# Steps of older images placed from written tables, one ring of four PSUM banks, and the second halves of the turned attention rows copied by VectorE

## The chip, the cores and the metric

The kernel runs on one core of a Trainium2 chip. The metric is the device time of one execution in microseconds (us). Three executions of the kernel before took 2924.77, 2925.54 and 2934.96 us; the median is 2925.54 us.

## What is computed

Eight images x of 128 channels and 32 x 32 points pass through six layers, each added to its input:

```python
x = x + deform_conv2d(_gn(x))          # group norm, 3x3 taps sampled at learned offsets
x = x + attention_conv(_gn(x))         # 1024 x 1024 attention, small q and k
t = to_tokens(x)                       # 1024 tokens of 128 channels
t = t + attention(_ln(t))              # scores + fractional log bias, softmax
t = t + experts(_ln(t))                # 8 experts, top 2 shares: gelu(t W1 + b1) W2 + b2
t = t + linear_attention(_ln(t))       # 16 heads, normed k and v, projection, gelu
t = t + experts(_ln(t))
```

All is float32. One image is one sequence of 1024 tokens, which the kernel holds as 8 tiles of 128 tokens.

## The kernel before

**Images overlap.** `period(m, p)` runs ten times (p from 0 to 9). In it image p, the front, goes through the deformable convolution (`sampling`), its projections (`mid0`), attention 1, `mid1` and attention 2. Beside it run *side steps* of older and of the next image: `experts(..., 0, ...)` (layer 2's experts, called A here) and `gating` of image p-1, `layer3`, `gating` B and `experts` B of image p-2, and `start` (group norm, offsets, the hat tables) of image p+1. From p = 2 to p = 6 all of them are there; in the periods 8 and 9 there is no front.

**Hooks.** The front's code calls `side(n)` at numbered places, the hooks. G hooks 0 to 52 lie in sampling (0 to 39) and `mid0` (40 to 52); X hooks 0 to 77 lie in attention 1 (0 to 32, three for each row tile j), `mid1` (33 to 44) and attention 2 (45 to 77). Each engine (PE, DVE, ACT, POOL, SP) has its own program with the same hooks and does its own share of a step there, so the order on every engine is written out; there is no scheduler. The list `..._PLACES[n]` names the steps at hook n. `placed` spreads the steps evenly between anchors.

**Experts.** A step of `experts` is a product into one PSUM bank (`hidden`, L820) with a gelu by ACT (L1077); at every odd step from 3 on also `outputs` (L830, 16 matrix instructions), which DVE weighs and adds to the tokens (L1404).

**An attention row tile j.** PE computes 128 x 1024 scores into a bank pair (L796), DVE takes the maximum (`nmax`, L1365), ACT the exponentials (`prob`, L1061). Two tiles later PE transposes them in two halves (`turn`, L780), ACT copies each half out of bank `pt` (`keep_turned`, L1047) and three tiles later PE multiplies by the values (`weigh`, L788). Gelu and exponential need different activation tables: an ACT_TABLE_LOAD stands at each change.

**Banks.** Four banks are shared, `pt`, `pv`, `3a` and `3b`. `shared_banks` goes through the hooks once and gives each product the bank that was used longest ago; in the X hooks only three, `pv`, `3a` and `3b`, since `pt` is kept for `turn`. PE waits in `claim` until the last reader of the bank has released it:

```python
def turn(j, h):
    claim("pt")
```

**Sampling.** 18 halves n = 2k, 2k+1 of 9 taps k. For each half the DMA queue of SP loads y hats into slot n % 4 of `dist`, and for each tap x hats into slot k % 2 of `prob`, four DMAs each; DVE multiplies them (`multiplied`, L1267); PE contracts the product with weighted image chunks (L670). DVE multiplies half n+1 before it goes through the two hooks of half n. `next_hats(m, n)` on SP waits until PE has used half n, asks for y hats n+4, and for odd n then waits for DVE's half n and asks for x hats of tap k+2.

## Time and profile before

| | |
|---|---|
| three runs | 2924.77 / 2925.54 / 2934.96 us |
| profiled execution, its own time | 2928.26 us |
| its span on the core | 2926.4 us |
| mean granted TensorE clock | 0.938 of full |
| busy PE / DVE / ACT | 2368.4 / 1429.6 / 1343.8 us |

The span is what the trace covers, from the first instruction to the last; 1.9 us of the profiled execution lie around it. An engine's busy time is the union of its instructions, so span less busy time is idle time, and a row in square brackets or a row of the waits says which instruction of which engine ended an idle stretch.

### The profile page before, as it was taken

The page shows a single profiled execution, that of the slowest core. Times are in us where ns is not written, and L with a number is a line of the kernel's source. Part 1 is how long each engine was busy: PE and PEld are TensorE (multiplying, and loading weights), DVE is VectorE, ACT ScalarE, POOL GpSimd, SP SyncE. Part 2 cuts the span into 40 slices and gives each one's busy share as a digit, 9 for nine tenths or more (in the row PEclk, how much of TensorE's full clock was granted, in tenths as well). Part 3 has the DMA queues.
Part 4 walks back from the last instruction along what each step waited for, and adds up shares of the span by engine and source line. Part 5 has one row for each costly group of instructions (what it writes and reads, how often), then busy time and mean ns, then how long its engine had stood idle before and what let it go on. Part 6 is the DMA issues. An engine that isn't in the chain of part 4 may idle for free.

```text
span 2926.4 us, 36546 instructions
## 1 busy us (share of the span) xinstructions
PE 2368.4 (81%) x12672; PEld 1738.2 (59%) x12672; DVE 1429.6 (49%) x3543; ACT 1343.8 (46%) x1784; POOL 93.8 (3%) x87
## 2 busy tenths in 40 slices
PE   4677787778978888787888888887897888977958
PEld 2555565566656665665656666566665666655646
DVE  2345345564446535465444644456453653455352
ACT  2135163426473365625565264742747337543323
POOL 0000000000000000000000000000000000000000
PEclk8889998989999999999999999998999999998979
DMA  8603600440005200170002600044000530000000
GB/s 276 140 1 87 152 1 7 119 113 1 1 37 137 73 1 8 53 174 13 1 15 80 145 8 1 29 108 109 1 1 37 136 67 1 1 8 1 1 8 8
DMA packets 106607, 157.88 MB, mean 54 GB/s; under 512 B 14896, under 2 KB 88720, under 8 KB 105872
## 3 DMA queue, kind: packets, MB, share of 16 engines
q1 hardware_dynamic: 104544, 142.39, 19.4%
q10 hardware_dynamic: 1840, 12.71, 1.1%
q8 instruction: 117, 1.92, 0.3%
q14 instruction: 106, 0.87, 0.1%
HBM read 126.76 MB, written 28.28 MB: 53 GB/s over the span
## 4 chain that ended last, share of the span: by engine, by line
PE 51%; ACT 16%; DVE 12%; ACTq 7%; issue 5%; DVEq 3%; DMA 3%; SPq 2%; PEld 0%; POOL 0%; PEldq 0%; POOLq 0%
PE pair L820 10%; PE pair L830 10%; PE pair L788 7%; PE pair L670 4%; ACT L1077 4%; ACT L1061 4%; ACTq L1063 4%; PE pair L657 3%; ACT dist L1047 3%; PE pair L780 3%; DMA prob<-hats 3%; ACTq L1078 3%; PE pair L603 2%; PE pair L617 2%; PE pair L796 2%
## 5 line engine op out<-in xcount | busy, mean ns | idle before, releaser
L670 PE MATMUL pair<-dist,thirds 128*128 128x256 f32 (+6 forms) x1440 | 315.6, 368 | 79.4 <-DVE dist L1267 71.7
L788 PE MATMUL pair<-vt,dist 128*128 128x128 f32 x2048 | 274.7, 291 | 90.5 <-ACT hiddenA L1077 45.3
L670 PEld LDWEIGHTS pair<-dist,thirds 128*128 128x128 f32 x1440 | 262.3, 209 | 136.9 <-DVE dist L1267 61.9
L788 PEld LDWEIGHTS pair<-vt,dist 128*128 128x128 f32 x2048 | 259.8, 205 | 118.1 <-issue 108.3
L830 PEld LDWEIGHTS pair<-wtsb,hiddenB 128*128 128x128 f32 x2048 | 251.8, 194 | 78.3 <-issue 50.5
L1077 ACT ACTIVATE hiddenB<-pair,wtsb 128x512 f32<-128x512 f32 x256 | 175.7, 687 | 257.0 <-PE pair L820 251.8
L820 PE MATMUL pair<-tnTB,wtsb 128*128 128x512 f32 x512 | 267.5, 617 | 30.4 <-ACT hiddenB L1077 26.8
L830 PEld LDWEIGHTS pair<-wtsa,hiddenA 128*128 128x128 f32 x2048 | 250.6, 194 | 67.7 <-issue 60.5
L820 PE MATMUL pair<-tnTA,wtsa 128*128 128x512 f32 x512 | 277.1, 634 | 9.8 <-ACT hiddenA L1077 6.2
L1077 ACT ACTIVATE hiddenA<-pair,wtsa 128x512 f32<-128x512 f32 x256 | 176.0, 687 | 223.4 <-PE pair L820 213.1
L1404 DVE SCALAR_TENSOR_TENSOR tokC<-pair,cwb,tokC 128x128 f32<-128x128 f32 x512 | 144.3, 345 | 262.6 <-PE pair L830 260.7
L1047 ACT ACTIVATE dist<-pair 128x512 f32<-128x512 f32 x256 | 152.9, 597 | 248.8 <-PE pair L780 236.0
L830 PE MATMUL pair<-wtsb,hiddenB 128*128 128x128 f32 x2048 | 253.3, 277 | 15.7 <-ACTq L1078 15.7
L830 PE MATMUL pair<-wtsa,hiddenA 128*128 128x128 f32 x2048 | 252.5, 277 | 0.1
L1267 DVE TENSOR_TENSOR dist<-dist,prob 128x1024 f32<-128x1024 f32 x144 | 174.6, 1223 | 135.6 <-DMA prob<-hats 113.9
L1365 DVE TENSOR_REDUCE nmax<-pair 128x1 f32<-128x1024 f32 x128 | 156.6, 1224 | 162.7 <-PE pair L796 161.0
L1404 DVE SCALAR_TENSOR_TENSOR tokD<-pair,cwa,tokD 128x128 f32<-128x128 f32 x448 | 126.2, 345 | 223.5 <-PE pair L830 222.7
L780 PE MATMUL pair<-early_sb,prob 128*128 128x128 f32 x1024 | 163.4, 282 | 65.7 <-ACT dist L1047 58.8
L993 ACT ACTIVATE thirds<-pair 128x768 f32<-128x768 f32 x96 | 77.9, 811 | 273.6 <-PE pair L657 273.2
L780 PEld LDWEIGHTS pair<-early_sb,prob 128*128 128x128 f32 x1024 | 120.1, 144 | 115.3 <-ACT dist L1047 100.8
L1061 ACT ACTIVATE prob<-pair,nmax 128x1024 f32<-128x1024 f32 x128 | 142.7, 1115 | 42.1 <-DVE nmax L1365 38.8
L1077 ACT ACT_TABLE_LOAD x120 | 154.0, 1283 | 16.1 <-issue 15.2
(193 smaller groups left out, 2923.8 us busy)
## 6 DMA issues: line engine op xcount, KB each, us to landing
dist<-hats SPq DMA_DIRECT2D x576, 128.0 KB, 3.3
prob<-hats SPq DMA_DIRECT2D x288, 128.0 KB, 3.4
hats<-dist SPq DMA_DIRECT2D x40, 512.0 KB, 2.7
ximg<-x SPq DMA_DIRECT2D x8, 512.0 KB, 3.8
result<-xo ACTq DMA_DIRECT2D x8, 512.0 KB, 3.9
hats<-prob SPq DMA_DIRECT2D x5, 608.0 KB, 15.0
late_sb<-late ACTq DMA_DIRECT2D x1, 2737.5 KB, 12.5
wtsa<-wa ACTq DMA_DIRECT2D x1, 2056.0 KB, 18.5
```

Of the source, the lines that this page charges most:

```text
L670: last = pe.matmul(pair[0][:, a:b], z[k // 3 % 2][:, c, k % 3, :], rhs(a, b), start=bank not in opened, stop=final, skip_group_check=True)
L780: last = pe.transpose(psum["pt"][:, t * P:(t + 1) * P], pr[j % 3][:, (4 * h + t) * P:(4 * h + t + 1) * P], ident)
L788: last = pe.matmul(psum[bank][:, 0:P], prT[j % 2][:, t, :], vt[:, t, :], start=(t == 0), stop=(t == NT - 1))
L820: pe.matmul(psum[bank], w[:, at_:at_ + P], xT[:, h * 512:(h + 1) * 512], start=True, stop=True)\
L830: last = pe.matmul(psum[bank][:, j * P:(j + 1) * P], hid[l][2 * (u % 2) + c][:, j * P:(j + 1) * P], w[:, at_:at_ + C], start=(c == 0), sto ...
L1047: released(act.activation(to, psum["pt"], ACT.Copy), "pt")
L1061: released(act.activation(pr[j % 3], pair[j % 2][:, :], ACT.Exp, bias=nmax[:, j:j + 1], accum_out=rsum[:, j:j + 1]), str(j % 2))
L1063: act.drain().then_inc(sem("prob_exp"), 1)
L1077: released(act.activation(hid[l][2 * (u % 2) + c], psum[bank], ACT.Gelu, bias=wts[l][:, at_:at_ + 1]), bank)
L1267: dve.tensor_tensor(slot, slot, windows(k, half), ALU.mult).then_inc(sem("hat_ready"), 1)
L1365: dve.tensor_reduce(nmax[:, j:j + 1], pair[j % 2][:, :], AX.X, ALU.max, negate=True)\
L1404: last = dve.scalar_tensor_tensor(to[:, t, :], psum[bank][:, j * P:(j + 1) * P], cw[l][:, t, e:e + 1], src[:, t, :], ALU.mult, ALU.add)
```

## The change

Four things are changed. The arithmetic is the same.

1. `placed` takes a written table: the hook of each step, one by one. Some steps now share a hook, and some stretches have none. `EARLY_EXPERTS` goes from 10 to 11: one more step of experts A lies in the G hooks.
2. The ring in the X hooks has all four banks, and the two halves of each turned tile take theirs from it, as every other product does.
3. The second half of each turned tile is copied by DVE, after the hook 3j+1, and no more by ACT.
4. In sampling DVE multiplies up to two halves ahead, by the table `MULTIPLY_AT` (entry i is the half n at which half i is multiplied), and SP asks for the x hats of tap k+2 before the y hats of half n+4.

```diff
+MULTIPLY_AT = [-1, 0, 0, 1, 2, 3, 4, 6, 6, 8, 8, 9, 10, 12, 13, 14, 15, 16]
+RING = ("pt", "pv", "3a", "3b")
+KEEP = ("act", "dve")
...
-def placed(anchors, hooks):
-
-    at = [[] for _ in range(hooks)]
-    for (s0, h0), (s1, h1) in zip(anchors, anchors[1:]):
-        for step in range(s0, s1):
-            at[h0 + (step - s0) * (h1 - h0) // (s1 - s0)].append(step)
-    return at
+def placed(first, at, hooks):
+
+    return [[first + n for n, h in enumerate(at) if h == hook] for hook in range(hooks)]
...
-EARLY_EXPERTS = 10
-EXPERTS_A_G_PLACES = placed([(0, 38), (EARLY_EXPERTS, G_HOOKS)], G_HOOKS)
-EXPERTS_A_PLACES = placed([(EARLY_EXPERTS, 0), (EXPERT_STEPS, 34)], X_HOOKS)
+EARLY_EXPERTS = 11
+EXPERTS_A_G_AT = [32, 34, 34, 40, 40, 42, 43, 46, 46, 51, 52]
+EXPERTS_A_G_PLACES = placed(0, EXPERTS_A_G_AT, G_HOOKS)
+EXPERTS_A_AT = [1, 2, 3, 3, 3, 3, 3, 8, 8, 8, 15, 16, 18, 19, 21, 22, 24, 24, 25, 26, 29, 31, 32]
+EXPERTS_A_PLACES = placed(EARLY_EXPERTS, EXPERTS_A_AT, X_HOOKS)
...
             for step in places[n]:
-                take(("pv", "3a", "3b"), claims(thread, l, step))
+                take(RING, claims(thread, l, step))
         for a, first in enumerate((0, ATTENTION2_AT)):
             i, r = divmod(n - first, 3)
             if r == 0 and 3 <= i < NT + 3:
-                take(("pv", "3a", "3b"), [("pv", a, i - 3)])
+                take(RING, [("pv", a, i - 3)])
+            if r < 2 and 2 <= i < NT + 2:
+                take(RING, [("turned", a, i - 2, r)])
...
             def next_hats(m, n):
 
-                if n + SLOTS < HALVES:
-                    sp.wait_ge(sem("hat_used"), at(m, HALVES, n + 1))
-                    load_hy(m, n + SLOTS)
                 k = n // 2
                 if n % 2 and k + 2 < TAPS:
                     sp.wait_ge(sem("hat_ready"), at(m, HALVES, n + 1))
                     load_hx(m, k + 2)
+                if n + SLOTS < HALVES:
+                    sp.wait_ge(sem("hat_used"), at(m, HALVES, n + 1))
+                    load_hy(m, n + SLOTS)
...
                 def turn(j, h):
-                    claim("pt")
+                    bank = SHARED["turned", a, j, h]
+                    claim(bank)
...
                 multiplied(0)
                 for n in range(HALVES):
-                    if n + 1 < HALVES:
-                        multiplied(n + 1)
+                    for later_half in range(1, HALVES):
+                        if MULTIPLY_AT[later_half] == n:
+                            multiplied(later_half)
...
+                def keep_turned(j, h):
+                    dve.wait_ge(sem("prob_T"), inst(m, a, 2 * NT, 2 * j + h + 1))
+                    if h == 0:
+                        dve.wait_ge(sem("pv"), inst(m, a, NT, j + 1))
+                    to = prT[j % 2][:, 4 * h:4 * h + 4, :].rearrange("p a b -> p (a b)")
+                    bank = SHARED["turned", a, j, h]
+                    released(dve.tensor_copy(to, psum[bank]), bank)
+                    dve.drain().then_inc(sem("probT_kept"), 1)
...
                     side(3 * j + 1)
+                    if KEEP[1] == "dve" and 2 <= j < NT + 2:
+                        keep_turned(j - 2, 1)
```

**ACT in the middle of attention 1.** The names: `prob` is the exponential, `hiddenA` a gelu of experts A, `dist` the copy of a turned half. Before:

```order
L1061 ACT_TABLE_LOAD
L1061 ACTIVATE prob,rsum<-pair,nmax 128x1024
L1077 ACT_TABLE_LOAD
L1077 ACTIVATE hiddenA<-pair,wtsa 128x512 x2
L1047 ACTIVATE dist<-pair 128x512 x2
L1061 ACT_TABLE_LOAD
L1061 ACTIVATE prob,rsum<-pair,nmax 128x1024
L1077 ACT_TABLE_LOAD
L1077 ACTIVATE hiddenA<-pair,wtsa 128x512 x2
L1047 ACTIVATE dist<-pair 128x512
L1077 ACTIVATE hiddenA<-pair,wtsa 128x512
L1047 ACTIVATE dist<-pair 128x512
```

Each tile has two table loads, two gelus and two copies. After the change (line numbers are those of the changed file):

```order
L1072 ACTIVATE prob,rsum<-pair,nmax 128x1024
L1088 ACT_TABLE_LOAD
L1088 ACTIVATE hiddenA<-pair,wtsa 128x512 x3
L1058 ACTIVATE dist<-pair 128x512
L1072 ACT_TABLE_LOAD
L1072 ACTIVATE prob,rsum<-pair,nmax 128x1024
L1058 ACTIVATE dist<-pair 128x512
L1072 ACTIVATE prob,rsum<-pair,nmax 128x1024
L1088 ACT_TABLE_LOAD
L1088 ACTIVATE hiddenA<-pair,wtsa 128x512
L1058 ACTIVATE dist<-pair 128x512
L1088 ACTIVATE hiddenA<-pair,wtsa 128x512
```

The copies of second halves are gone, three gelus stand together, and between the last two exponentials of the piece there is no gelu and no table load.

**PE at the start of `mid0`.** L576 (now L585) is the group product that waits for DVE's statistics, L583 (now L592) the q and k projections, L820 and L830 (now L830 and L840) are experts A. Before:

```order
L576 MATMUL pair<-gstF,early_sb 128x1
L617 MATMUL pair<-early_sb,tnB 128x128 x4
L820 MATMUL pair<-tnTA,wtsa 128x512 x2
L830 MATMUL pair<-wtsa,hiddenA 128x128 x8
L576 MATMUL pair<-gstF,early_sb 128x1
L858 MATMUL pair<-late_sb,tnTB 128x8 x4
L820 MATMUL pair<-tnTA,wtsa 128x512 x2
L830 MATMUL pair<-wtsa,hiddenA 128x128 x8
L583 MATMUL pair<-xrows,early_sb 128x512 x2
L820 MATMUL pair<-tnTA,wtsa 128x512
L583 MATMUL pair<-xrows,early_sb 128x512 x2
```

After:

```order
L840 MATMUL pair<-wtsa,hiddenA 128x128 x8
L830 MATMUL pair<-tnTA,wtsa 128x512
L585 MATMUL pair<-gstF,early_sb 128x1
L626 MATMUL pair<-early_sb,tnB 128x128 x4
L830 MATMUL pair<-tnTA,wtsa 128x512
L840 MATMUL pair<-wtsa,hiddenA 128x128 x8
L585 MATMUL pair<-gstF,early_sb 128x1
L868 MATMUL pair<-late_sb,tnTB 128x8 x4
L830 MATMUL pair<-tnTA,wtsa 128x512 x2
L840 MATMUL pair<-wtsa,hiddenA 128x128 x8
L830 MATMUL pair<-tnTA,wtsa 128x512
L592 MATMUL pair<-xrows,early_sb 128x512 x4
```

An outputs product and a hidden product now stand right ahead of the first group product (and one hidden product more ahead of this piece); two hidden products, an outputs product and a third hidden one stand right ahead of the projections, all four of which follow each other.

**DVE in the first half of sampling.** L1480 (now L1505) takes keys and values of the linear attention out of PSUM, L1487 to L1499 (now L1512 to L1524) norm them, L1267 (now L1278) multiplies hats. Before:

```order
L1448 TENSOR_TENSOR tnTF<-tnTF,late_sb 128x256
L1450 TENSOR_TENSOR tnTF<-tnTF 128x256
L1452 TENSOR_REDUCE cwa<-tnTF 128x32
L1454 SCALAR_TENSOR_TENSOR cwa<-cwa,lga 128x32
L1487 TENSOR_REDUCE hm<-hiddenA 128x128
L1267 TENSOR_TENSOR dist<-dist,prob 128x1024
L1458 COPY cwTa<-pair 64x128
L1494 TENSOR_SCALAR hm<-hm 128x256
L1496 RECIPROCAL hm<-hm 128x256
L1499 TENSOR_TENSOR qk<-qk,hm 128x1024
L1267 TENSOR_TENSOR dist<-dist,prob 128x1024
L1499 TENSOR_TENSOR qk<-qk,hm 128x1024
```

After:

```order
L1278 TENSOR_TENSOR dist<-dist,prob 128x1024
L1505 TENSOR_TENSOR qk<-pair,early_sb 128x512
L1512 TENSOR_REDUCE hm<-hiddenA 128x128 x2
L1519 TENSOR_SCALAR hm<-hm 128x256
L1521 RECIPROCAL hm<-hm 128x256
L1524 TENSOR_TENSOR qk<-qk,hm 128x1024 x2
L1483 COPY cwTa<-pair 64x128
L1278 TENSOR_TENSOR dist<-dist,prob 128x1024 x2
```

The norms are now one piece with no multiplication of hats inside it; two multiplications stand behind it. Before, two stand inside the piece shown and a third just ahead of it, between the last L1480 and the first L1487.

## Rows read from the trace of the kernel before

**Rows 1.** The page, part 1: busy us of each engine and its share

```profile
PE 2368.4 (81%) x12672; PEld 1738.2 (59%) x12672; DVE 1429.6 (49%) x3543; ACT 1343.8 (46%) x1784; POOL 93.8 (3%) x87
```

**Rows 2.** Windows by image: length, busy of each engine, granted clock, DMA share, GB/s

```profile
45.00:287.00 242.00, 172.22 (x818) 122.11 (x819) 102.61 (x199) 78.20 (x120) 6.06 (x6) 0.89 0.38 89
...
1241.00:1591.00 350.00, 292.28 (x1581) 216.25 (x1581) 177.32 (x440) 175.46 (x229) 11.12 (x10) 0.95 0.21 52
```

**Rows 3.** Windows of one full image: sampling, projections, attention 1, mid1, attention 2

```profile
1241.00:1328.00 87.00, 74.44 (x351) 56.87 (x350) 55.95 (x111) 23.78 (x31) 5.35 (x4) 0.94 0.67 158
1328.00:1365.00 37.00, 28.16 (x139) 18.93 (x139) 20.18 (x51) 15.73 (x20) 0.56 (x1) 0.86 0.05 16
1365.00:1433.00 68.00, 56.93 (x366) 44.60 (x365) 26.71 (x66) 51.53 (x65) 0.00 (x0) 1.00 0.00 1
1433.00:1479.00 46.00, 40.58 (x232) 29.10 (x232) 20.26 (x71) 13.45 (x21) 2.57 (x3) 0.96 0.00 1
1479.00:1591.00 112.00, 92.17 (x500) 66.76 (x501) 54.23 (x143) 70.97 (x94) 2.64 (x2) 0.94 0.10 34
```

**Rows 4.** Timeline of PE in attention 1: start, length, line, idle and releaser

```profile
1394.98 2.02 PE L788 MATMUL pair<-vt,dist 128*128 128x128 f32 x16 [1.55 <-ACT hiddenA L1077]
...
1398.13 0.66 PE L780 MATMUL pair<-early_sb,prob 128*128 128x128 f32 x4 [0.69 <-ACT dist L1047]
...
1399.08 1.02 PE L796 MATMUL pair<-k,q 128*128 128x512 f32 x2
1399.94 1.02 PE L820 MATMUL pair<-tnTA,wtsa 128*128 128x512 f32 x2
...
1404.30 2.02 PE L788 MATMUL pair<-vt,dist 128*128 128x128 f32 x16 [1.55 <-ACT hiddenA L1077]
```

**Rows 5.** Timeline of ACT in the same tile

```profile
1399.51 1.28 ACT L1061 ACT_TABLE_LOAD   x1
1400.81 1.12 ACT L1061 ACTIVATE prob<-pair,nmax 128x1024 f32<-128x1024 f32 x1
...
1402.17 1.28 ACT L1077 ACT_TABLE_LOAD   x1 [0.15 <-issue]
1403.46 0.69 ACT L1077 ACTIVATE hiddenA<-pair,wtsa 128x512 f32<-128x512 f32 x1
```

**Rows 6.** Groups of ACT by line: count, busy, mean ns, idle before

```profile
L1077 ACT ACT_TABLE_LOAD x120 | 154.0, 1283 | 16.1 <-issue 15.2 <-PE pair L830 0.4
L1047 ACT ACTIVATE dist<-pair 128x512 f32<-128x512 f32 x256 | 152.9, 597 | 248.8 <-PE pair L780 236.0 <-issue 5.5
```

**Rows 7.** Groups of DVE by line

```profile
L1267 DVE TENSOR_TENSOR dist<-dist,prob 128x1024 f32<-128x1024 f32 x144 | 174.6, 1223 | 135.6 <-DMA prob<-hats 113.9 <-DMA dist<-hats 14.6 <-issue 2.7
L1365 DVE TENSOR_REDUCE nmax<-pair 128x1 f32<-128x1024 f32 x128 | 156.6, 1224 | 162.7 <-PE pair L796 161.0
...
L1517 DVE TENSOR_TENSOR hiddenB<-pair,tnTB 128x512 f32<-128x512 f32 x16 | 11.0, 689 | 25.7 <-PE pair L603 25.7
```

**Rows 8.** Waits of PE, first stage of the projections: total, times, longest

```profile
PE pair L576 <- DVE gstF L1188: 6.5, 1, 6.5
PE pair L583 <- DVE xrows L1205: 2.4, 1, 2.4
```

**Rows 9.** Waits of PE between the attentions

```profile
PE pair L796 <- issue: 3.2, 1, 3.2
```

**Rows 10.** Waits of PE in the sampling

```profile
PE pair L670 <- DVE dist L1267: 7.4, 5, 3.8
```

**Rows 11.** Timeline of DVE in the sampling

```profile
1270.55 0.69 DVE L1480 TENSOR_TENSOR qk<-pair,early_sb 128x512 f32<-128x512 f32 x1 [0.62 <-PE pair L893]
...
1282.57 1.22 DVE L1499 TENSOR_TENSOR qk<-qk,hm 128x1024 f32<-128x1024 f32 x1
```

**Rows 12.** Waits of PE in the first 562 us

```profile
PE pair L670 <- DVE dist L1267: 31.7, 14, 5.7
PE pair L780 <- ACT dist L1047: 22.2, 28, 1.7
```

## What the change does to the time

> **What bounds the kernel now.** I read part 1 of the page first. PE is busy for 2368.4 us of 2926.4, DVE for 1429.6, ACT for 1343.8 [rows 1]. The change leaves PE's products as they are, so what it can win is PE's idle time, 558 us. The windows by image say where it is: 70 us in the first image (242.00 less 172.22) and 58 in a full one (350.00 less 292.28) [rows 2]. Five images are full (p = 2 to 6); a sixth lacks the next image.
>
> The windows by stage split these 58 us: 12.6 in sampling, 8.8 in the projections, 11.1 in attention 1, 5.4 in `mid1`, 19.8 in attention 2 and its end [rows 3]. No stage has an engine that is busy all the time, so waits form rings. The timelines show one in attention 1. `weigh` of one tile starts at 1394.98 and of the next at 1404.30: a tile takes 9.32 us. In it PE waits 1.55 us ahead of `weigh` for a gelu, which holds the bank that `weigh` takes from a ring of three, and 0.69 us ahead of the second `turn`, whose only bank ACT's copy of the first half holds [rows 4]. ACT meanwhile loads tables: one load starts at 1399.51, the exponential at 1400.81, the next load at 1402.17 [rows 5]. Both waits of PE, 2.24 us, end with ACT, and without them PE needs 7.08 us for a tile.
>
> **What each part costs or gives.**
>
> *Table loads.* The order of ACT's instructions has 263 loads before and 211 after; in a full image 39 and 31. One lasts 1283 ns [rows 6]: 52 of them are 66.7 us of ACT's time. The exponential starts 1.30 us after its load starts [rows 5], so nothing but the load itself goes with it. The Trainium skill (ScalarE: Activation LUTs, What ACT_TABLE_LOAD costs) gives 1283 ns and a drain of about 1380 ns more for a switch. By it, an estimate, 52 loads would be 138 us of ACT; the trace agrees on the load and shows no such drain ahead of the exponential.
>
> *Second halves.* 128 copies leave ACT, 128 x 0.597 = 76 us [rows 6]. The trace has no copy of 512 columns out of PSUM on VectorE. Below, it is bounded by ACT's 0.597, above by the reduction of 1024 columns, 1.224 us; the addition of 512 columns, nearest in shape, took 0.689 [rows 7]. I take 0.69: 88 us, and DVE comes to some 1520. Queued behind the copy on DVE is `nmax` of the next tile, which ACT waits for. But PE makes that tile's scores only after the second `turn`, in 0.86 us (1399.08 to 1399.94) [rows 4], and 0.69 lies beside them. So I cost it at nothing; with that cover gone it is 88 us in all, or 157 at 1.224.
>
> *Ring of four, attention 1.* Both waits lose their cause: the second `turn` has a bank of its own, and there is a bank more between a gelu and `weigh`. In a tile with two hidden products ACT then needs two loads to the next start (2.6), the exponential (1.36), two gelus of 0.69 [rows 5], one copy of 0.60 and half a microsecond of gaps, 6.4 us; PE needs 7.08 and sets the pace. In the two tiles without experts the chain is `weigh`, two turns and DVE's copy, some 0.3 us longer than PE's own work. Of 11.1 us idle I leave 2: 9 won.
>
> *Entry into attention 2.* PE waits 3.2 us for DVE [rows 9], which is held by the first offsets product. Experts and the second offsets product now stand in that gap. 3 won.
>
> *Attention 2.* Here `start`'s hat tables add to ACT, busy for 71 us of 112 against 92 of PE [rows 3]. It loses 8 copies and 4 loads, 10 us. Tiles with tables and without experts now bunch, and there ACT sets the pace; the bound is from nothing to 19.8 us, and I take a third, 7.
>
> *Projections.* PE waits 6.5 us for statistics and 2.4 for the normed image [rows 8]. An outputs product is 16 instructions like `weigh`, up to 2.0 us, a hidden one has the length of the scores, 0.86 [rows 4]; one and two of them now stand ahead of each wait, 3.7 us. Up to 3.7 + 2.4 could go; I take 5.
>
> *Sampling.* PE waits 7.4 us for products of hats, once 3.8 [rows 10]; DVE in turn waits 113.9 us in the whole run for x hats [rows 7]. On SP these no more stand behind y hats whose request waits for PE, so they leave up to one half earlier, 87/18 = 4.8 us, and most of the 7.4 should go. The y hats of odd halves start four DMA issues later, beside a half more of lead. The price is on DVE: the norms of keys and values now stand in one piece. From 1270.55 to 1283.79 it took 13.2 us [rows 11]. Less three hat products of 1.22 [rows 7] and some 2 us of gating, both no more inside, 7.6 are left. Behind it are queued the hats of halves 7 and 8; PE has one ready half and one chunk, some 3 us, then waits 7.6 + 1.2 - 3 = 6 us. Given and taken, 1 won.
>
> A full image wins 9 + 3 + 7 + 5 + 1 = 25 us, five of them 125. The sixth has no entry wait and less to win in attention 2: 20. In the first two images PE waits 31.7 us for hats and 22.2 for the copy of the first half, 28 times [rows 12]. The separate bank ends nearly all of the second, the earlier request perhaps a third of the first: 30. The last two periods keep their order and get a bank: 2. Sum 177. From the profiled execution's own 2928.3 that gives 2751; the median of the three runs, 2925.5, is 2.7 lower, so 2748 on its scale, and I say 2750.
>
> **Rivals.** A difference under 0.5% (15 us) can't be told from no change here.
>
> - *The forecast*: 0.60, with a range of its own from 2700 to 2815. The low end lets every full image win 29 us, as if nothing were left of the named waits but ACT's pace in attention 2, and the first two all 54: 145 + 24 + 54 + 3 = 226. The high end is 110 us won.
> - *Sampling takes most back.* Each bunch of older steps holds a hat product behind it, and PE's clock falls after a wait: 0.86 granted in the stage with the 6.5 us wait, 1.00 in attention 1 [rows 3]. If a full image loses 10 more there and the sixth too, 177 - 60 = 117, and with the first images' hats unchanged about 100: 2828. For it: no hat product inside DVE's piece. Against it: the 7.4 us that go. Chance 0.13.
> - *VectorE's copies are not hidden.* 88 us come back through `nmax`: 2750 + 88 = 2838. For it: each second `turn` now ends in a wait of DVE, in order. Against it: DVE idles 58 of 112 us in attention 2 and 41 of 68 in attention 1 [rows 3]. Chance 0.13.
> - *Nothing is gained.* The loads lay beside PE's work anyhow, and a bunch of gelus can hold four banks as it held three: 2926, chance 0.05.
> - *Slower: DVE's piece starves PE and its clock stays low.* PE loses the 9 us of the piece, and the 35 us of its work in the rest of sampling run at 1.2 instead of 2.4 GHz. That is up to 44 in each of six images, 264 against 177 won: 3010 at most. It turns the sign once a full image loses 29 us there, so with the low clock for 20 us. I put 2970. Chance 0.09.
>
> Faster: 0.60 + 0.13 + 0.13 = 0.86; same 0.05; slower 0.09. The range reaches from 2690, 10 us below the forecast's own low end for clock that PE regains, to 2865, which holds both middle rivals; it leaves out the last two cases and a little at each end.
>
> **What would show it.** (a) 211 loads, ACT's busy time near 1344 - 67 - 76 = 1200, DVE's near 1520, a copy near 0.69. (b) No waits of PE for ACT's first-half copy, a tile of attention 1 with two hidden products at 7.1 us instead of 9.32, 2 us idle in the stage. (c) No 3.2 us wait ahead of the first scores of attention 2. (d) About 4 us left of the two waits in the projections. (e) In sampling PE's waits caused by late x hats gone, a new one of 6 us behind DVE's norms. (f) A full image takes 325 us. The forecast is wrong if (f) stays above 340 with (b) as told: then the gain was lost in another stage, which the windows name. It is wrong too if ACT waits longer for `nmax`, behind the copies.

## The result and the profile after

The changed kernel takes 2528.8 us (median of 4 runs, 2527.6 to 2530.1), the kernel before in the same session 2929.7 (4 runs). The ratio is 0.863, with a 95% interval from 0.861 to 0.865: 401 us less, where 177 were forecast (2750, range 2690 to 2865). The sign and the named waits were right. The size was not, and the time lies outside the range.

Part 1 of the page, as in [rows 1]:

```profile
PE 2254.3 (89%) x12672; PEld 1692.2 (67%) x12672; DVE 1522.2 (60%) x3671; ACT 1199.4 (47%) x1604; POOL 98.4 (4%) x87
```

The span is 2528.2 us, so PE's idle time fell from 558 to 274 us. The same row shows a second thing: PE executes the same 12672 products as before and is busy 114 us less. The forecast took that number as fixed.

The windows by image (columns as in [rows 2]), the first two, one full one, the sixth and the last two periods:

```profile
47.00:260.00 213.00, 164.16 (x794) 120.14 (x794) 107.28 (x191) 64.27 (x98) 4.16 (x5) 0.86 0.39 91
260.00:498.00 238.00, 205.18 (x1151) 153.63 (x1151) 138.83 (x317) 103.22 (x142) 6.79 (x7) 0.98 0.32 72
...
1078.00:1369.00 291.00, 273.15 (x1581) 207.00 (x1581) 188.43 (x457) 155.56 (x205) 12.04 (x10) 0.99 0.24 62
...
1950.00:2248.00 298.00, 277.11 (x1607) 212.58 (x1606) 190.84 (x481) 147.33 (x194) 14.79 (x11) 0.98 0.20 49
2248.00:2528.00 280.00, 222.51 (x1176) 160.95 (x1176) 122.83 (x369) 93.01 (x129) 8.03 (x6) 0.87 0.01 4
```

A full image takes 291 us instead of 350, and PE waits in it for 18 us instead of 58. Its 1581 products take 273.15 us instead of 292.28, at a mean granted clock of 0.99 instead of 0.95 [rows 2]. The five full images gave 292 us together, the sixth 53, the first two 49, the last two periods 6, which is the 401 but for 1 us.

The full image of [rows 3] by stage, in the same order:

```profile
1078.00:1161.00 83.00, 71.66 (x349) 55.35 (x348) 55.99 (x109) 25.77 (x34) 6.26 (x4) 0.96 0.68 166
1161.00:1190.00 29.00, 24.43 (x139) 17.28 (x139) 21.20 (x59) 13.14 (x16) 0.56 (x1) 1.00 0.06 20
1190.00:1244.00 54.00, 53.64 (x354) 43.06 (x353) 30.46 (x69) 42.34 (x55) 0.00 (x0) 1.00 0.01 1
1244.00:1287.00 43.00, 43.00 (x264) 32.29 (x263) 24.42 (x86) 13.44 (x20) 2.57 (x3) 1.00 0.00 1
1287.00:1369.00 82.00, 80.43 (x481) 59.01 (x480) 56.36 (x136) 60.87 (x82) 2.65 (x2) 1.00 0.13 44
```

The reader is to see two things. From attention 1 to the end of attention 2 PE now waits 1.9 us in 179 us (36.3 in 226 before): these stages are bound by PE. And the granted clock is 1.00 wherever those waits were; of the five stages only sampling is still below it. (Attention 1 has 12 instructions fewer than in [rows 3], attention 2 has 19 fewer and `mid1` 32 more: products that the tables moved there. So the three lengths are best read together: 226 us before, 179 now.)

The tile of attention 1 with two hidden products, which took 9.32 us in [rows 4], as a timeline of PE:

```profile
1219.93 1.95 PE L798 MATMUL pair<-vt,dist 128*128 128x128 f32 x16
1221.72 0.60 PE L790 MATMUL pair<-early_sb,prob 128*128 128x128 f32 x4
1222.16 1.02 PE L830 MATMUL pair<-tnTA,wtsa 128*128 128x512 f32 x2
1223.02 0.60 PE L790 MATMUL pair<-early_sb,prob 128*128 128x128 f32 x4
1223.38 0.71 PE L806 MATMUL pair<-k,q 128*128 128x512 f32 x2
1223.92 1.02 PE L830 MATMUL pair<-tnTA,wtsa 128*128 128x512 f32 x2
1224.78 1.95 PE L840 MATMUL pair<-wtsa,hiddenA 128*128 128x128 f32 x16
1226.57 1.95 PE L798 MATMUL pair<-vt,dist 128*128 128x128 f32 x16
```

It takes 6.64 us, without a wait. The forecast was 7.08, what PE's products took when the two waits were subtracted; 0.44 us more went. In a row of products each starts before the one ahead has ended; ahead of a wait the last one runs to its end, and behind it the first weights are loaded with no product beside them. So the outputs product took 1.95 us to the wait and takes 1.79 (1224.78 to 1226.57) to the next start, and `weigh` took 1.86 behind its wait and takes 1.79. The two waits of this tile cost 0.22 us each beyond their length.

The groups by line that answer to [rows 6] and [rows 7]:

```profile
L1088 ACT ACT_TABLE_LOAD x94 | 120.6, 1283 | 12.5 <-issue 11.6 <-PE pair L840 0.6
L1058 ACT ACTIVATE dist<-pair 128x512 f32<-128x512 f32 x128 | 76.4, 597 | 122.0 <-PE pair L790 117.6 <-issue 4.4
```

```profile
L1278 DVE TENSOR_TENSOR dist<-dist,prob 128x1024 f32<-128x1024 f32 x144 | 174.1, 1223 | 106.9 <-DMA prob<-hats 51.0 <-DMA dist<-hats 49.5 <-issue 3.1
L1386 DVE TENSOR_REDUCE nmax<-pair 128x1 f32<-128x1024 f32 x128 | 156.6, 1224 | 29.9 <-PE pair L806 22.8
L1379 DVE COPY dist<-pair 128x512 f32<-128x512 f32 x128 | 88.5, 691 | 40.7 <-PE pair L790 32.5 <-issue 1.1
```

### The profile page after: what moved, and what is told of

It is laid out like the page before. It is cut to its first block, busy times and chain, and to the rows that moved or that the text cites. A ratio compares the mean times of both kernels' runs of the same rounds, so it can differ in the third digit from the quotient of the medians.

```text
span 2528.2 us, 36494 instructions
## 1 busy us (share of the span) xinstructions
PE 2254.3 (89%) x12672; PEld 1692.2 (67%) x12672; DVE 1522.2 (60%) x3671; ACT 1199.4 (47%) x1604; POOL 98.4 (4%) x87
## 4 chain that ended last, share of the span: by engine, by line
PE 72%; DVE 12%; ACT 5%; issue 3%; DVEq 2%; DMA 2%; ACTq 1%; SPq 1%; PEld 1%; POOL 1%; PEldq 0%; POOLq 0%
PE pair L840 17%; PE pair L830 16%; PE pair L798 8%; PE pair L679 7%; PE pair L666 4%; PE pair L806 4%; PE pair L790 3%; PE pair L612 2%; PE pair L640 2%; DVE dist L1278 1%; DMA prob<-hats 1%; PE pair L884 1%; PE pair L619 1%; PE pair L626 1%; PE pair L868 1%
## 5 line engine op out<-in xcount | busy, mean ns | idle before, releaser
L679 PE MATMUL pair<-dist,thirds 128*128 128x256 f32 (+6 forms) x1440 | 296.6, 355 | 74.8 <-DVE dist L1278 69.6
L679 PEld LDWEIGHTS pair<-dist,thirds 128*128 128x128 f32 x1440 | 250.8, 199 | 129.0 <-DVE dist L1278 68.7
L840 PEld LDWEIGHTS pair<-wtsa,hiddenA 128*128 128x128 f32 x2048 | 252.5, 194 | 71.1 <-issue 59.7
L840 PEld LDWEIGHTS pair<-wtsb,hiddenB 128*128 128x128 f32 x2048 | 247.1, 192 | 59.2 <-issue 50.6
L798 PEld LDWEIGHTS pair<-vt,dist 128*128 128x128 f32 x2048 | 245.1, 194 | 48.8 <-DVEq L1380 35.9
L830 PE MATMUL pair<-tnTA,wtsa 128*128 128x512 f32 x512 | 259.6, 603 | 15.0 <-issue 12.6
L798 PE MATMUL pair<-vt,dist 128*128 128x128 f32 x2048 | 257.3, 280 | 15.8 <-DVEq L1380 15.8
L840 PE MATMUL pair<-wtsa,hiddenA 128*128 128x128 f32 x2048 | 253.8, 278 | 7.1 <-DVE tokD L1429 6.6
L830 PE MATMUL pair<-tnTB,wtsb 128*128 128x512 f32 x512 | 253.7, 605 | 3.1 <-DVE tokC L1429 1.4
L840 PE MATMUL pair<-wtsb,hiddenB 128*128 128x128 f32 x2048 | 249.6, 275 | 0.0
L1278 DVE TENSOR_TENSOR dist<-dist,prob 128x1024 f32<-128x1024 f32 x144 | 174.1, 1223 | 106.9 <-DMA prob<-hats 51.0
L666 PE MATMUL pair<-early_sb,xrows 128*128 128x384 f32 x384 | 153.4, 524 | 8.2 <-ACT thirds L1003 8.2
L790 PE MATMUL pair<-early_sb,prob 128*128 128x128 f32 x1024 | 146.9, 275 | 8.6 <-ACT dist L1058 2.7
L830 PEld LDWEIGHTS pair<-tnTB,wtsb 128*128 128x128 f32 x512 | 87.3, 192 | 73.6 <-issue 58.4
```

Of the source, the lines that this page charges most:

```text
L666: last = pe.matmul(pair[1][:, 512 * c:512 * c + 384], xn[:, (2 * d + c) * P:(2 * d + c + 1) * P], const("w0")[:, t * 384:(t + 1) * 384], s ...
L679: last = pe.matmul(pair[0][:, a:b], z[k // 3 % 2][:, c, k % 3, :], rhs(a, b), start=bank not in opened, stop=final, skip_group_check=True)
L790: last = pe.transpose(psum[bank][:, t * P:(t + 1) * P], pr[j % 3][:, (4 * h + t) * P:(4 * h + t + 1) * P], ident)
L798: last = pe.matmul(psum[bank][:, 0:P], prT[j % 2][:, t, :], vt[:, t, :], start=(t == 0), stop=(t == NT - 1))
L830: pe.matmul(psum[bank], w[:, at_:at_ + P], xT[:, h * 512:(h + 1) * 512], start=True, stop=True)\
L840: last = pe.matmul(psum[bank][:, j * P:(j + 1) * P], hid[l][2 * (u % 2) + c][:, j * P:(j + 1) * P], w[:, at_:at_ + C], start=(c == 0), sto ...
```

## The experiments

Two theories stood against each other at first: that the places of the older steps carry the gain (each tile's ACT work then fits beside PE's), or that the fourth bank and VectorE's copies do. Two more were that the 52 table loads themselves were on the path, and that a wait of PE costs its granted clock besides its length. What a part is worth is the median without it less the changed kernel's 2528.8, or, for a part alone, the median of the kernel before in the same session less that with the part. The medians of the kernel before lie between 2929.7 and 2937.9 in all sessions, so differences of a few us between sessions mean nothing. Diffs are against the changed kernel.

### One part undone

**All older steps spread evenly again.** The tables of places go back to the rule of before (`placed_evenly`, the removed function):

```diff
-EXPERTS_A_PLACES = placed(EARLY_EXPERTS, EXPERTS_A_AT, X_HOOKS)
+EXPERTS_A_PLACES = placed_evenly([(EARLY_EXPERTS, 0), (EXPERT_STEPS, 34)], X_HOOKS)
...
```

> The changed kernel with the older images' steps spread evenly again, as before (263 table loads); ring of four, VectorE's copies and early x hats stay. If the placing carries most of the 401 us, this loses 250 or more: 2780 us or above, full image near 335 us, PE idle near 450 us. If the bank and the copies carry most, it loses at most 120: 2650 or below. If most of the gain is the granted clock that follows from PE's short waits, then besides the idle time PE's own busy time rises, from 2254 to above 2320.

**ACT copies both halves.**

```diff
-KEEP = ("act", "dve")
+KEEP = ("act", "act")
```

> The changed kernel with ACT copying both halves of the turned rows (second halves back from VectorE). If ACT paced the tiles before and its load is what counted, each full image loses about 16 x 0.6 us where ACT is the bound: 2570 to 2610. If the copies lie beside PE's work on either engine: 2529 to 2540. If VectorE's copies are not hidden (rival of the prediction), this is faster: 2480 or below.

**Ring of three and one bank for turned halves.**

```diff
+X_RING = ("pv", "3a", "3b")
...
-                take(RING, claims(thread, l, step))
+                take(X_RING, claims(thread, l, step))
...
-                take(RING, [("turned", a, i - 2, r)])
+                banks["turned", a, i - 2, r] = "pt"
```

> The changed kernel with a ring of three banks in the X stages and the turned halves in one bank of their own, as before; new places, VectorE's copies and early x hats stay. If the bank is what ended PE's waits ahead of the second turn, the wait comes back: 0.7 us in each of 8 tiles of 14 attentions and more behind gelus, 2610 to 2650. If the placing alone keeps banks free, 2540 or below.

**Hats as before.**

```diff
-MULTIPLY_AT = [-1, 0, 0, 1, 2, 3, 4, 6, 6, 8, 8, 9, 10, 12, 13, 14, 15, 16]
+MULTIPLY_AT = [-1] + list(range(17))
...
+                if n + SLOTS < HALVES:
+                    sp.wait_ge(sem("hat_used"), at(m, HALVES, n + 1))
+                    load_hy(m, n + SLOTS)
                 k = n // 2
                 if n % 2 and k + 2 < TAPS:
                     sp.wait_ge(sem("hat_ready"), at(m, HALVES, n + 1))
                     load_hx(m, k + 2)
-                if n + SLOTS < HALVES:
-                    sp.wait_ge(sem("hat_used"), at(m, HALVES, n + 1))
-                    load_hy(m, n + SLOTS)
```

> The changed kernel with x hats asked for behind y hats again and the products of hats one half ahead. If the hats carry only what the windows of sampling show (4 us in each of 8 images): 2555 to 2570. If PE's short waits in sampling also cost its granted clock, 60 us or more: 2590 or above. If they are hidden: 2529.

### One part alone

The same edits combined: the kernel before with the new places alone, with ring and copies alone, with the hats' order alone.

> The kernel before with the new places of the older steps alone (211 table loads; ring of three, both copies on ACT, old hats). Taken from the changed kernel they were worth 226 us. If the parts add up: 2930 - 226 = 2705. If bunched steps need the fourth bank (three hidden products in a row and pv are four claims), they win less alone, under 150: 2780 or above. If ring and copies only pay behind the new places, they win more alone, 2650 or below.

> The kernel before with the ring of four and VectorE's copies alone. From the changed kernel ring and copies were worth 86 and 49 us. If the parts add up: 2930 - 135 = 2795. If the bank matters most to bunched steps, the evenly spread ones win less from it: 2850 or above.

> The kernel before with the hats' new order alone. It was worth 49 us from the changed kernel. If it adds up: 2881. If the waits of sampling are replaced by those behind VectorE's norms, it wins under 20: 2910 or above.

What the seven measured:

| kernel | median us | ratio to before, 95% | what the part is worth, us |
|---|---|---|---|
| places undone | 2754.5 | 0.938 (0.935 to 0.942) | 226 |
| ACT copies both | 2578.0 | 0.878 (0.875 to 0.881) | 49 |
| ring of three | 2614.4 | 0.891 (0.887 to 0.894) | 86 |
| hats as before | 2578.1 | 0.879 (0.875 to 0.883) | 49 |
| places alone | 2741.2 | 0.934 (0.930 to 0.937) | 191 |
| ring and copies alone | 2771.5 | 0.945 (0.942 to 0.948) | 161 |
| hats alone | 2902.1 | 0.989 (0.986 to 0.993) | 30 |

Undone one by one the parts are worth 410 us, alone 382, in all 401: in total they add up. Single parts do so only within 35 us: alone, the places won 35 us less than their loss when undone, ring and copies 26 us more, the hats 19 less. No part lives by another. The places carry about half (191 to 226 us) and ring and copies a third or more (135 to 161), so neither of the first two theories holds alone. The expectation of 250 or more for the places was missed by 24; its last case came true, for with the places undone PE's busy time is 2322.6 us, 68 more for the same products. ACT's copies and the ring fell into their first cases, the hats (49 us where 26 to 41 or 61 and more were expected) into none.

Where each part works is read from the windows of attention 1 and attention 2 in the fourth image. First the kernel after, then places undone, ACT copying both, the ring of three:

```profile
898.00:965.00 67.00, 66.64 (x454) 54.65 (x453) 38.83 (x100) 45.55 (x59) 1.01 (x1) 1.00 0.01 1
...
995.00:1077.00 82.00, 80.37 (x480) 58.83 (x479) 56.08 (x135) 60.86 (x82) 2.65 (x2) 1.00 0.12 43
```

```profile
978.00:1047.00 69.00, 67.12 (x452) 54.48 (x451) 38.41 (x101) 50.67 (x63) 1.01 (x1) 1.00 0.01 1
...
1079.00:1176.00 97.00, 87.39 (x502) 63.80 (x500) 59.48 (x151) 66.20 (x86) 2.65 (x2) 0.96 0.11 39
```

```profile
909.00:978.00 69.00, 66.99 (x454) 54.67 (x453) 33.31 (x92) 50.30 (x67) 1.01 (x1) 1.00 0.00 1
...
1009.00:1097.00 88.00, 81.10 (x477) 58.51 (x476) 50.66 (x128) 65.63 (x90) 2.65 (x2) 1.00 0.11 39
```

```profile
930.00:1003.00 73.00, 67.90 (x455) 54.43 (x454) 39.15 (x101) 45.53 (x59) 1.01 (x1) 1.00 0.00 1
...
1034.00:1118.00 84.00, 79.83 (x478) 58.65 (x477) 56.13 (x135) 60.84 (x82) 2.65 (x2) 1.00 0.12 43
```

The bank works mostly in attention 1 (73 us against 67), the copies mostly in attention 2 (88 against 82), and the places mostly in attention 2 (97 against 82, of which some 5 us of products stand in `mid1` after) and ahead of attention 1 (119 against 110). With the ring of three the wait of PE for ACT's copy of the first half is back, 64 times in the run:

```profile
PE pair L791 <- ACT dist L1059: 54.4, 64, 1.5
```

### Which of the places

Three kernels, each with some tables spread evenly again and the others new.

> The changed kernel with only the experts' steps of both older images spread evenly again (211 table loads stay). All places together were worth 226 us. If the tiles' pace is set by where the gelus stand, most of it is here: 2680 or above. If it is set by the table loads, which start's hats and the gatings share, little of it is: 2600 or below.

> The changed kernel with only the steps of the next image's start and of the early gating and third layer spread as before (211 table loads). If attention 2, which the prediction sized at a third of its idle time, owes its gain to these: 2600 or above. If to the experts: 2550 or below.

> The changed kernel with only the third layer's and the gatings' steps of the G stages spread as before. If the products ahead of the projections' two waits cover them, as the prediction has it, 5 us come back in each of 6 images, and their clock: 2560 to 2590. If VectorE's one piece of norms cost 6 us an image in sampling, spreading it gives that back: 2529 or below.

| spread evenly again | median us | ratio, 95% | worth, us |
|---|---|---|---|
| experts of both images | 2663.9 | 0.908 (0.905 to 0.911) | 135 |
| next image's start, early gating, early layer 3 | 2617.7 | 0.892 (0.889 to 0.895) | 89 |
| layer 3 and gatings of the G stages | 2541.3 | 0.866 (0.863 to 0.869) | 12 |

They sum to 236 for the 226 of all. The experts' 135 lie below the expected 151 and are still the largest part. They are not free of the table loads, as the expectation had it: with the experts spread ACT executes 52 instructions more (1656 against 1604) and is busy 66.3 us more, so all 52 loads come back with them. `start`'s steps are worth 89 us and keep all 211 table loads: with them spread, the first two images' attention 2 takes 63.6 us instead of 52.4 on the mean, a full one 92.6 instead of 81.9. So attention 2 doesn't owe its gain to the experts alone. With the experts spread a full image loses 17 us: 7 in attention 2, 3 in attention 1 and 7 ahead of it, where sampling and projections together take 118 us instead of 111. Only the experts' table of the G stages changes what stands in that last stretch, so that table is the cover ahead of the projections' waits. The layer 3 and gating tables gave back 12 us, between the cases expected. Two things are summed in these 12: with VectorE's norms no more in one piece PE waits 27.6 us for products of hats instead of 69.6, but 58 instead of 15 for two operands that VectorE makes in these steps (32.9 for `qk` of layer 3, 25.4 for `cwa` of the gating).

### Are the table loads on the path?

The changed kernel with 64 more gelus of one column that nothing reads, one behind each exponential of attention 1:

```diff
                         act.drain().then_inc(sem("prob_exp"), 1)
+                        if j in ((0, 1, 2, 3, 4, 5, 6, 7), ())[a]:
+                            act.activation(spare[0:18, :], const("ones")[:, 0:1], ACT.Gelu)
```

> The changed kernel with one gelu of a single column, of an unused tile, behind each exponential of attention 1: 255 table loads against 211, 44 x 1.28 = 56 us of ACT. If the loads that went were on the path, much of this shows, 40 us or more: 2570 or above. If ACT has room in attention 1 behind the new places (ACT had 0.36 us waits ahead of it only in tiles without experts): 2529 to 2545.

```profile
L1077 ACT ACTIVATE spare<-early_sb 18x1 f32<-18x1 f32 x64 | 12.9, 202 | 0.7
```

```profile
912.00:982.00 70.00, 66.93 (x454) 54.53 (x453) 38.84 (x100) 51.32 (x71) 1.01 (x1) 1.00 0.00 1
```

2561.0 us, ratio 0.873 (0.870 to 0.876): 32 us for 44 loads (56.5 us) and 12.9 us of gelus, so 0.46 us for each us put on ACT. At that rate, an estimate, the 52 loads that went were worth some 31 us; only attention 1 was tried, not attention 2. The 32 us lie between the two cases expected. By this the loads are a part of the places' gain, and of the experts' 135 us, and not the bulk.

### Does a wait cost more than its length?

The changed kernel with one needless wait in each tile of attention 2:

```diff
                         last.then_inc(sem("energy"), 1)
+                        if a:
+                            pe.wait_ge(sem("nmax"), inst(m, a, NT, j + 1))
```

> The changed kernel with one more wait in attention 2 alone: after its own scores of each tile PE waits for VectorE's maximum of them, at least the 1.2 us of the reduction in each of 56 tiles, so 67 us of idle at the least, and the same products. If a wait costs only itself: 2529 + about 75 = 2600 to 2620, PE's busy time stays at 2254. If short waits also take PE's clock down (the term that the prediction left out), PE's busy time rises too, by 20 us or more, and the time passes 2630.

Attention 2 of the fourth image, to be set beside the second window of the kernel after above:

```profile
1037.00:1136.00 99.00, 84.54 (x479) 60.83 (x478) 56.05 (x134) 61.17 (x82) 2.65 (x2) 0.97 0.10 36
```

```profile
PE 2286.3 (86%) x12672; PEld 1707.0 (64%) x12672; DVE 1522.0 (57%) x3671; ACT 1201.1 (45%) x1604; POOL 98.4 (4%) x87
```

2649.9 us, ratio 0.903 (0.900 to 0.906): 121 us more. PE's idle time rose by 90.5 us (273.9 to 364.4) and its busy time, for the same products, by 32.0 (2254.3 to 2286.3). Each us of waiting cost 1.34 by the medians, 1.35 within the profiled executions. The window shows both: 82 us became 99, 4.2 of the 17 as busy time, and the clock fell from 1.00 to 0.97. The theory holds. The expected 56 tiles were 64.

The other kernels show that 1.35 is no constant. The same quotient, one plus the busy time over the idle time that came with it, and the two things that could make up the busy time, against the kernel after:

| kernel | idle, us | busy, us | quotient | busy at 1.2 GHz, us | more waits over 0.3 us |
|---|---|---|---|---|---|
| needless waits | +90.5 | +32.0 | 1.35 | +54 | 48 |
| places undone | +149.1 | +68.3 | 1.46 | +103 | 56 |
| ring of three | +67.3 | +16.8 | 1.25 | +7 | 65 |
| ACT copies both | +42.3 | +6.0 | 1.14 | -16 | 46 |
| hats as before | +35.8 | +11.4 | 1.32 | +21 | 7 |
| kernel before | +284.1 | +114.1 | 1.40 | +144 | 185 |

Half of the fifth column, which the full 2.4 GHz would have saved, plus 0.22 us for each wait of the last gives 38, 64, 18, 2, 12 and 113 us for the 32, 68, 17, 6, 11 and 114 measured. The ring of three adds short waits (1.5 us at most for the copy) and hardly any time at the lower clock, the hats as before add time at the lower clock and hardly any waits, so the two prices stand nearly alone in these two.

### Sampling: the predicted wait, and its end

The 6 us wait behind VectorE's norms came as forecast. PE's products with halves 7 and 8 of the hats, and one later group of ten of them, in the kernel after:

```profile
1120.43 3.78 PE L679 MATMUL pair<-dist,thirds 128*128 128x64 f32 x10 [6.28 <-DVE dist L1278]
...
1130.33 2.00 PE L679 MATMUL pair<-dist,thirds 128*128 128x64 f32 x10
```

A group of ten such products takes 3.78 us behind the wait and 2.00 later. On VectorE the stretch reads:

```profile
1111.42 2.35 DVE L1512 TENSOR_REDUCE hm<-hiddenA 128x128 f32<-128x1024 f32 x2
1114.25 0.29 DVE L1519 TENSOR_SCALAR hm<-hm 128x256 f32<-128x256 f32 x1 [0.48 <-ACT hm L1125]
1114.63 1.75 DVE L1521 RECIPROCAL hm<-hm 128x256 f32<-128x256 f32 x1
1116.46 2.36 DVE L1524 TENSOR_TENSOR qk<-qk,hm 128x1024 f32<-128x1024 f32 x2
...
1119.15 2.36 DVE L1278 TENSOR_TENSOR dist<-dist,prob 128x1024 f32<-128x1024 f32 x2
```

Next, this piece was cut in two, and then in four, each also in a second version with the product of half 7 asked one half earlier (`MULTIPLY_AT[7] = 5`); PE's order is that of the changed kernel in all. In two:

```diff
-LAYER3_AT = [0, 1, 2, 2, 2, 2, 9, 11, 11, 11, 15, 15, 15, 15, 15, 15, 17, 19, 23, 25, 26, 26, 26, 28, 28, 28, 28, 29, 29]
+LAYER3_AT = [0, 1, 2, 2, 2, 2, 9, 11, 11, 11, 15, 15, 15, 15, 17, 17, 17, 19, 23, 25, 26, 26, 26, 28, 28, 28, 28, 29, 29]
```

> The changed kernel with VectorE's one piece of norms cut in two: the reciprocal of the third layer's norms and the scaling by it stand one half later, behind the products of halves 7 and 8; PE's order is untouched. If PE's wait of 6.3 us in sampling is due to this piece, 4 to 5 us go in each of 6 images, and half of the 5 us that PE is busy at 1.2 GHz behind it: 2529 less 25 to 45, 2484 to 2504. If the next late product takes its place: 2520 or above.

> The same with the product of half 7 also asked one half earlier, ahead of the whole piece. If PE still waited for it behind the first half of the piece: 2 us an image more won, 2475 to 2495. If its hat is then not yet in and VectorE stops for the transfer: no better than the cut piece, or worse.

And in four:

```diff
-LAYER3_AT = [0, 1, 2, 2, 2, 2, 9, 11, 11, 11, 15, 15, 15, 15, 15, 15, 17, 19, 23, 25, 26, 26, 26, 28, 28, 28, 28, 29, 29]
+LAYER3_AT = [0, 1, 2, 2, 2, 2, 9, 11, 11, 11, 15, 15, 15, 15, 17, 17, 19, 21, 23, 25, 26, 26, 26, 28, 28, 28, 28, 29, 29]
-MULTIPLY_AT = [-1, 0, 0, 1, 2, 3, 4, 6, 6, 8, 8, 9, 10, 12, 13, 14, 15, 16]
+MULTIPLY_AT = [-1, 0, 0, 1, 2, 3, 4, 6, 6, 7, 8, 9, 10, 12, 13, 14, 15, 16]
```

> The changed kernel with VectorE's norms of the third layer in four parts, and a product of hats between each two: the scaling one half later (hook 17), the weights and biases at hooks 19 and 21 instead of 17 and 19, the product of half 9 one half earlier; PE's order is untouched. The cut in two only moved PE's wait, from 6.3 us to 1.2 + 5.2 behind the joined rest. If the wait is queueing behind whichever piece is longest, no piece is now over 5 us against 4 us that PE needs for a half: PE's wait falls below 2.5 us, 4 us in each of 6 images go, 2490 to 2510. If VectorE as a whole (its busy time in these halves) is what PE waits for, the wait stays, in parts: 2520 or above.

> The same, and the product of half 7 one half earlier, ahead of the first piece. If its hat is in by then, PE has a half more in hand: some 2 us an image below the other. If VectorE stops for the transfer: the same or slower.

| VectorE's norms | median us | ratio, 95% |
|---|---|---|
| one piece (the kernel after) | 2528.8 | 0.863 (0.861 to 0.865) |
| two | 2525.9 | 0.861 (0.859 to 0.863) |
| two, half 7 earlier | 2523.3 | 0.860 (0.858 to 0.862) |
| four | 2491.6 | 0.848 (0.847 to 0.850) |
| four, half 7 earlier | 2489.3 | 0.848 (0.846 to 0.849) |

The cut in two won 3 us instead of 25 to 45, and half 7 asked earlier won 3 more instead of 2 in each image: both expectations fell into their second case. The timeline of PE shows why: the wait moved one half on, to where the rest of the piece had joined the norms behind it.

```profile
1112.84 2.00 PE L679 MATMUL pair<-dist,thirds 128*128 128x64 f32 x10 [1.23 <-DVE dist L1278]
...
1125.46 3.78 PE L679 MATMUL pair<-dist,thirds 128*128 128x64 f32 x10 [5.21 <-DVE dist L1278]
```

In four parts the wait of 5.21 us is gone and the one of 1.23 stays (timeline of PE, same image):

```profile
1099.40 2.00 PE L679 MATMUL pair<-dist,thirds 128*128 128x64 f32 x10 [1.23 <-DVE dist L1278]
...
1106.73 2.00 PE L679 MATMUL pair<-dist,thirds 128*128 128x64 f32 x10
```

So it was queueing behind the longest piece and not VectorE's load, which is the same in all five (1519 to 1522 us busy). The version in four parts also asks for the product of half 9 one half earlier; what that gives alone wasn't tried. Sampling and projections of the fourth image, after and in four parts:

```profile
788.00:898.00 110.00, 96.03 (x490) 72.99 (x489) 78.17 (x169) 39.18 (x49) 6.81 (x5) 0.97 0.54 130
```

```profile
778.00:882.00 104.00, 94.00 (x492) 71.11 (x490) 77.89 (x169) 39.16 (x49) 6.81 (x5) 1.00 0.61 139
```

6 us an image: 4 of waiting, 2 of clock (0.97 to 1.00). This version beats the changed kernel by 37 us, or 1.5%. Over the whole run PE is idle 24.6 us less and busy 14.6 us less, with 30 us less at 1.2 GHz and 4 waits more: here the clock alone makes up the busy time, and each us of waiting gave 1.6 us. The earlier half 7 adds 2 us, which can't be told from nothing.

**Which half of the hats' change.** The changed kernel with x hats first and the products one half ahead:

```diff
-MULTIPLY_AT = [-1, 0, 0, 1, 2, 3, 4, 6, 6, 8, 8, 9, 10, 12, 13, 14, 15, 16]
+MULTIPLY_AT = [-1] + list(range(17))
```

> The changed kernel with the hats' products one half ahead again but the x hats still asked for first. Both together were worth 49 us. If late x hats were what cost sampling, nearly nothing comes back: 2529 to 2540. If the products' places carry it: 2560 to 2580.

2531.5 us, ratio 0.863 (0.861 to 0.866). The request for x hats carries nearly all of the 49 us, the places of the products nothing that can be measured. PE's waits for products, after and with the hats as before:

```profile
PE pair L679 <- DVE dist L1278: 69.6, 27, 6.3
```

```profile
PE pair L679 <- DVE dist L1278: 107.4, 39, 6.3
```

## Why the prediction was wrong in size

The waits that it named went, for the causes that it gave. Two things failed: a term that was missing from the sum, and the reason and size of the step for attention 2. Of the 398 us between the two profiled executions 284 are idle time and 114 busy time of PE; the sum had 177 and none. So the shortfall is 107 us of idle time (75 of it in the five full images) and 114 us of busy time.

- **The first step, "what it can win is PE's idle time, 558 us", failed.** PE's busy time fell by 114 us. Two prices of a wait beyond its length make it up. One is the clock: summed over the trace's record of it, PE was busy for 284 us at the lower level, 1.2 GHz, before, and for 140 after; half of the difference, 72 us, is lost time that came back. The other is 0.22 us at each wait, for the product that runs out and the weights that load alone: waits over 0.3 us fell from 353 to 168, and 185 x 0.22 is 41 us, an estimate from one tile's 0.44. 72 + 41 = 113. The clock was in the prediction as a danger (the slower rival) and in 10 us at the low end, not as a gain, although [rows 3] showed 0.94 in attention 2 and 0.86 in the projections. The needless waits show the mechanism on the chip, and the same two prices give the busy time of all six kernels of the table above to within 6 us. The division is worked out from the traces; no run changed the clock by itself.
- **Attention 2, "I take a third, 7", failed.** Idle time in the stage fell from 19.8 to 1.6 us, the upper bound all but reached. The reason given for a third, that steps bunch and "there ACT sets the pace", was wrong: ACT is busy 61 of 82 us, PE 80.4. Before, each of the tiles 3 to 6 of this stage (of 0 to 7, from scores to scores) had two or three gelus and two or three of the instructions that make hat tables, and PE waited 1.7 to 3.0 us in each. Now tiles 4 and 6 have hat tables and no gelu and last 5.0 and 5.7 us without a wait of PE; tile 5 has six gelus and three tables, ACT busy 14.2 of its 16.2 us, and PE waits 0.2. That the gain needs both tables is shown by the 89 us of `start`'s and the 135 of the experts'; that it comes from such a split is read from these tiles. I read the bunches one by one, as load, and not against what else ACT does in that tile. Copies were part of it too: with ACT making them all, the stage has 6.9 us of idle time.
- **Attention 1, 9**: idle fell by 10.7, to 0.4 where 2 were to stay. The waits at `weigh` and at the second `turn` went, and a tile takes 6.64 us. The mechanism is right; besides what was counted there are the 0.44 us of each such tile. (b) held with a shorter tile.
- **Entry into attention 2, 3**: the wait of [rows 9] is gone, as (c) says. That DVE held it is not in the row, which has "issue". It cost more than its 3.2 us: the four score instructions behind it took 3.39 us, where they take 1.88 without it.
- **Projections, 5**: 37 us became 29, 8 won. Of the two waits, 8.9 us, 1.6 of the first is left and nothing of the second; with smaller waits beside them PE's idle time in the stage went from 8.8 to 4.6 us, near (d)'s 4, and its clock from 0.86 to 1.00. The cover was the experts' products of the G table, as the step has it.
- **Sampling, 1**: 87 us became 83. The new wait of 6.3 us is there, for the 6 of the step, with its place and cause, and VectorE's piece takes the 7.6 us forecast (1111.42 to 1119.01). What was too small is the other side: the hats' new order is worth 49 us in all, 6 in a full image, nearly all of it by the earlier request. VectorE's waits for x hats fell from 113.9 to 51.0 us, and those for y hats rose from 14.6 to 49.5.
- **Table loads** are 211, ACT is busy 1199 us (forecast 1200), VectorE 1522 (1520), the copy 691 ns (0.69): (a) held to the digit. The Trainium skill (ScalarE: Activation LUTs, What ACT_TABLE_LOAD costs) adds a drain of about 1380 ns to each change of tables; by it, an estimate, the 44 loads put in would be 117 us of ACT instead of 56. No row shows such a drain, and the whole kernel rose by 32 us.
- **VectorE's copies** are hidden, for the reason given: ACT's copies undone cost 49 us, and `nmax` did not become a wait that matters. That rival would have given 88 us back. The rival in which sampling takes most back had its wait and not its price, since the x hats paid more.
- **First two images, 30**: 49, of which 43 idle time. **Sixth, 20**: 53, of which 35 idle time and 18 busy. **Last two periods, 2**: 6.
- **The range** took over the same fault. Its bound for attention 2 was 19.8 and its low end let a full image win 29 us, not the 38 that the bounds gave (25 - 7 + 20), and the clock 10 us in all. By the bounds it is 38 x 6 + 54 + 3 = 285 us of idle time, where 284 went; this is worked out afterwards, and that it meets to 1 us is partly luck, since the bounds take the sixth image as full.

In a full image the sum was 9 + 3 + 7 + 5 + 1 = 25. It came out at 59 in the image of [rows 3]: 40 us of waits and 19 of busy time, of which some 14 are clock: PE was busy at 1.2 GHz for 32.8 us of such an image before and for 5.2 after.

## What to carry to other kernels

Price a wait of TensorE at more than its length, here 1.14 times where the waits were short and left the clock alone, up to 1.6 times where they took it down, and read the granted clock of each stage as time to be won back where a change removes the waits. When steps are placed by hand, judge the bunches by the sum of what each engine does in that stretch, not by the count of steps; a bunch is no load if its neighbour on the engine has moved away. When a long piece in an engine's queue starves another engine, cut it until no part is longer than what the consumer has in hand: here one cut only moved the wait, three left 1.2 us of it.

## What the runs showed of the hardware

- TensorE's products behind a wait: ten that take 2.00 us took 3.78 behind a wait of 6.28 us and again behind one of 5.21, and 2.00 behind one of 1.23. In attention 2 of the kernel before it was the same with 16 products that take 1.95 us elsewhere (timeline of PE below). Waits of up to 1.8 us in attention 1 of the kernel before left the clock at 1.00 [rows 3]. In attention 2 of the kernel with needless waits (1037 to 1136 us) PE waited 1.91 us once and 2.48 once, each time beside a stretch at 1.2 GHz, while the waits of 1.32 us, and one of 2.07, had none.
- A copy of 128 x 512 out of PSUM takes VectorE 691 ns and ACT 597.
- PE's busy time is no property of its products alone: the same 12672 instructions took 2368.4 us before, 2254.3 after and 2239.7 with the norms in four parts.
- A gelu of one column on 18 partitions takes ACT 202 ns; the load at a change of tables is 1283 ns in all of these kernels.

```profile
1557.11 3.52 PE L788 MATMUL pair<-vt,dist 128*128 128x128 f32 x16 [2.50 <-ACT hiddenB L1077]
...
1569.66 3.00 PE L788 MATMUL pair<-vt,dist 128*128 128x128 f32 x16 [2.01 <-ACT hiddenB L1077]
```
